# Moving a short normalisation chain on VectorE, and its transpose on TensorE, within a hand-ordered attention and routed-FFN kernel

## The chip, the cores and the metric

One core of a Trainium2 chip. The metric is device time in microseconds of one execution. The engines are named as in the profile: PE (TensorE), DVE (VectorE), ACT (ScalarE), POOL (GpSimd), SP (SyncE, which issues the transfers here).

## The reference

The input x has 16 batches of 512 tokens of 128 values. Two layers follow each other, and each is added to its input and normalised:

```
x = layernorm(x + attention(x))            # 16 heads of 8, causal, capped scores
x = layernorm(x + routed_ffn(x))           # 63 of 512 tokens per batch

# routed_ffn, for the chosen tokens of a batch:
weights = x @ router_w + router_b          # one weight for each token
k = 64; thr = 64th largest weight; sel_idx = sorted indices of the 63 largest
x_sel, w_sel, m_sel = rows of x, weights, mask at sel_idx
hn = rmsnorm(x_sel) * ln1
q, kk = rope(hn @ wq), rope(hn @ wk);  v = hn @ wv
o  = softmax(q kk^T / sqrt(8) + m_sel) v @ wo
x1 = x_sel + o
x2 = x1 + gelu((rmsnorm(x1) * ln2) @ w1) @ w2
out = x2 * w_sel scattered to sel_idx; the other tokens pass through
```

The change concerns the line of x2: the normalisation of x1 (the second rmsnorm of this layer), and how its result reaches the product with w1.

## The kernel before, in words

Batches are worked on in pairs. A pair has slots for 2 x 64 chosen tokens, so the small attention of the routed layer (track "att", one unit for each pair) fills 128 partitions. The main attention (scores, capped softmax, product with v) runs batch by batch, in 8 groups of two heads. The program is one loop over iterations, each with 16 steps, one group of the main attention to a step; a step has two halves. In each half PE first computes a unit of scores into the PSUM tile ps_s (line 1182), which ACT turns into probabilities (tanh line 716, exp line 731), POOL masks (line 627) and PE uses (line 1199, track "pv").

All other work is hung onto these halves by hand: PE_ORDER, VE_ORDER, POOL_ORDER and ACT_ORDER are tables of 32 entries, one for each half. An entry such as "att.h2T@-2" calls a function for the pair two iterations back; "/0" or "/1" picks the batch of a pair. Each engine goes through its own table in order, and the engines meet only at semaphores: every step counts up its track's semaphore, and whoever needs the step waits for the count. On DVE the halves mean nothing but the order.

The steps that matter here, in order of the data:

- att.wo (PE, line 1382) writes the attention's output projection into the PSUM tile ps_a. att.x1f (DVE, line 1073) adds the chosen tokens' own values. att.ss (line 1077) sums squares. att.root1 (guess, a, t: lines 806, 808, 809) and att.root2 (u2, u3, u4, y: lines 811 to 814) are an inverse root by polynomial on a 128x1 tile, sel_v. att.hn (line 1082) scales the tokens into the tile hn.
- att.h2T (PE, line 1387) turns hn into ps_a, DVE copies it, scaled, to the tile h2T (line 1085), and att.w1 (PE, line 1393) multiplies by w1. DVE copies that to hb (line 1091).
- route.wrow (PE, line 1206) spreads the token weights of a batch over all partitions of the PSUM tile ps_m; route.row (DVE, line 939) copies it to w_wide; route.win (DVE, line 946, four instructions) compares. This belongs to another batch.
- fin.root1 and fin.root2 (DVE, the same lines 806 to 814, on ln_v, 128x4) are the inverse root of a layer norm of yet another batch; fin.x1 (line 922) uses it.
- prep.xT (PE, line 1223) turns the 512 tokens of the next pair's first batch into ps_m, and DVE copies them to xT (line 828).

Two PSUM banks, ps_a and ps_m, are shared by all these steps. A table says whose reading must be over before a step may write:

```
    "att.h2T": ["att.x1f@0"],
    "att.w1": ["att.h2T@0"],
    "prep.xT/0": ["prep.vb/1@-1", "route.row/0@-2"],
```

So prep.xT of the first batch, which writes ps_m, waits until DVE's route.row has read ps_m. The chains on DVE wait for their own previous step by semaphore; the copy route.row waits for PE's wrow.

Of the kernel before, what the change touches and what calls it, by code (L numbers as in the profile page):

```python
# [61 lines left out]
def moments_of(tiles, tag=""):  # L62
# [48 lines left out]
    ["fin.y1T/1@-1"], ["att.P1@-2", "fin.yT/1@-1", "att.PV@-2"],  # L111
    [], ["fin.wo/1@-1"],
    ["pv.0/0@0", "pv.1/0@0", "pv.2/0@0"], ["att.oT@-2"],
    ["pv.3/0@0", "att.wo@-2", "route.wrow/0@-1"], ["att.h2T@-2"],
    [], ["prep.xT/0@1", "att.w1@-2"],
    ["route.won/0@-1", "prep.qk0/0@1", "prep.qk1/0@1"], ["fin.y0T/0@0", "pv.4/0@0", "route.wrow/1@-1"],
    ["pv.5/0@0", "pv.6/0@0"], ["route.thr/0@-1", "pv.7/0@0", "route.won/1@-1"],
    ["prep.v/0@1"], ["fin.y1T/0@0", "late.w2@-2"],
# [9 lines left out]
    ["prep.qk0/1@0", "fin.x1/0@-1", "route.coef/1@-2", "att.den@-2", "prep.qk1/1@0"], ["fin.yU1/1@-1"],  # L128
    ["att.PT0@-2", "prep.v/1@0", "prep.ss/1@0", "fin.y1/1@-1"], ["att.PT1@-2", "prep.root1/1@0"],
    ["prep.root2/1@0", "prep.qkn/1@0", "fin.yT/1@-1", "late.ln@-3", "prep.hi/1@0"], ["route.w/0@-1"],  # L130
    ["att.o@-2", "fin.res/1@-1", "att.oT@-2", "fin.ln/1@-1"], ["route.row/0@-1", "att.x1f@-2"],
    ["att.ss@-2", "fin.root1/1@-1", "att.root1@-2", "att.root2@-2", "att.hn@-2"],
    ["fin.root2/1@-1", "route.win/0@-1", "att.h2T@-2"],
    ["late.root1@-3", "fin.x1/1@-1", "prep.xT/0@1"], ["att.h@-2", "route.w/1@-1", "fin.yU0/0@0"],
    ["route.rank/0@-1", "prep.qk0/0@1", "prep.qk1/0@1", "fin.y0/0@0"], ["att.hp@-2"],
# [1326 lines left out]
```

How the kernel before makes its waits and increments, by code:

```python
    def wait(self, eng, unit, name):  # L312
        pair, k = self.where(unit)
        if not isinstance(pair, int) or 0 <= pair < PAIRS:
            eng.wait_ge(self.sems[k], pair * len(self.names) + (self.names.index(name) + 1))
# [190 lines left out]
        @block.sync  # L507
# [31 lines left out]
            def turn(b, k):  # L539
                if b.at_least(2):
                    sp.wait_ge(scores_ready, (b - 1).no * 16)
                for s, (dst, part) in enumerate(((q_st, "q"), (k_st, "k"))):
                    pl["prep"].wait(sp, b, f"lo_{part}")
                    sp.dma_start_transpose(out=dst[:, k].rearrange("p g (t n) -> p (g t) n", t=NT),
                                           in_=st[:, s].rearrange("p g t j c d -> p (g t j c d)")).then_inc(turned[k], 16)
# [17 lines left out]
                if live(p, PAIRS):  # L564
                    load_res(Batch(p, 1), 1)
                if live(p + 1, PAIRS):
                    turn(Batch(p, 2), 0)
                if p in (1, 2):
                    pe["sel"].wait(sp, p - 1, "R")
                    load_mask(2 * p if p == 1 else MASKS - 1, mask_a[:, :, :])
                    if p == 1:
                        load_mask(MASKS - 1, mask_b)
            for k in range(2):
                sp.wait_ge(out_stored[k], 16 * PAIRS)
# [2 lines left out]
        @block.gpsimd  # L577
# [30 lines left out]
            nc.gpsimd.memset(v_aug[:, :, :, :, :], 0.0).then_inc(zeroed, 1)  # L608
            nc.gpsimd.memset(pm[:, :, :], 0.0).then_inc(zeroed, 1)
            pool.wait_ge(zeroed, 2)
            for s in range(2):
```

## Time and profile before

| | |
|---|---|
| runs shown | 831.39, 833.25, 834.76 us; median 833.25 us |
| the profiled execution | span 830.0 us from first to last instruction; its own device time is not listed beside it |
| busy share of the span | PE 82%, DVE 72%, ACT 67%, PE weight loads 48%, POOL 47% |
| chain of work that ended last | PE 61%, DVE 18%, issue 10%, ACT 7%, POOL 3%, DMA 1% |
| pairs in the routed track | 8, one for each of 8 iterations |

The chain of work that ended last is followed back from the last instruction; its shares tell on which engine time could be won or lost. The busy shares are means over the whole span. The granted clock of PE is 1.00 where it runs at 2.4 GHz and 0.50 where it runs at 1.2 GHz. A row of a timeline gives start, duration, engine, line, operation, tiles, and in brackets how long the engine had stood idle before it and who released it. Where a row has a count over one, several instructions are merged, and the duration is from the start of the first to the end of the last.

### The profile page before, as it was taken

What the parts mean: (1) busy time and instruction counts of PE and PEld (TensorE: products, weight loads), DVE (VectorE), ACT (ScalarE), POOL (GpSimd) and SP (SyncE); (2) the same over time, 40 slices, a digit from 0 to 9 for tenths busy, and PEclk for the clock granted to TensorE, in tenths of its full rate; (3) what the DMA queues carried; (4) which work ended last, traced back from release to release, by engine and by line L of the source; (5) the groups of instructions that cost most, each with busy time, mean ns of one, the idle gap of its engine ahead of it and who ended that gap; (6) DMA issues with size and microseconds to landing.
All of it is one profiled execution on the core that took longest, in us unless ns stands there. A gap on an engine that the chain in (4) does not pass through costs nothing.

```text
span 830.0 us, 16995 instructions
## 1 busy us (share of the span) xinstructions
PE 678.9 (82%) x6576; PEld 401.4 (48%) x6576; DVE 595.4 (72%) x1681; ACT 554.2 (67%) x403; POOL 392.0 (47%) x399
## 2 busy tenths in 40 slices
PE   3588787889979988999899988998899879865652
PEld 2344334455546455645455545645565535434232
DVE  4442718777787788958888788769896986588455
ACT  0588688889768876959768876788687968600000
POOL 5263436447544574346455664446546543421201
PEclk8567678899789987989789987899799979985755
DMA  6321302033300503030304030120303030000001
GB/s 190 64 42 37 64 13 53 25 61 119 64 14 17 112 12 67 27 64 14 64 14 90 14 64 15 50 54 2 64 26 65 2 64 27 13 1 26 0 0 51
DMA packets 96913, 36.75 MB, mean 44 GB/s; under 512 B 68018, under 2 KB 94146, under 8 KB 96834
## 3 DMA queue, kind: packets, MB, share of 16 engines
q1 hardware_dynamic: 96834, 35.67, 18.8%
q8 instruction: 53, 0.87, 0.4%
q14 instruction: 26, 0.21, 0.1%
HBM read 14.69 MB, written 4.19 MB: 23 GB/s over the span
## 4 chain that ended last, share of the span: by engine, by line
PE 61%; DVE 18%; issue 10%; ACT 7%; POOL 3%; DMA 1%; POOLq 0%; DVEq 0%; ACTq 0%
PE ps_y L1199 16%; PE ps_s L1182 14%; ACT pr L731 4%; PE ps_m L1308 3%; PE ps_m L1230 3%; ACT th L716 3%; PE ps_m L1206 3%; PE ps_a L1230 3%; PE ps_m L1356 2%; PE ps_a L1393 2%; DVE v_aug L844 2%; PE ps_m L1258 2%; PE ps_a L1206 2%; PE ps_a L1258 1%; PE ps_a L1292 1%
## 5 line engine op out<-in xcount | busy, mean ns | idle before, releaser
L716 ACT ACTIVATE th<-ps_s 128x1024 f32<-128x1024 f32 (+1 forms) x256 | 280.2, 1129 | 110.7 <-PE ps_s L1182 102.0
L627 POOL TENSOR_TENSOR pr<-pr,tri 128x320 f32<-128x320 f32 (+1 forms) x256 | 194.8, 784 | 186.7 <-ACT pr L731 186.7
L731 ACT ACTIVATE pr<-th 128x2304 f32<-128x2304 f32 x128 | 271.5, 2122 | 15.5 <-PE ps_y L1199 15.4
L1182 PE MATMUL ps_s<-q_st,k_st 32*64 32x512 f16 (+7 forms) x2048 | 193.1, 319 | 24.9 <-ACT th L716 20.8
L1199 PE MATMUL ps_y<-pr,v_aug 128*32 128x512 f32 (+7 forms) x2048 | 157.4, 439 | 0.4 <-POOL pr L627 0.4
L1182 PEld LDWEIGHTS ps_s<-q_st,k_st 32*64 32x64 f16 x2048 | 92.3, 114 | 120.0 <-issue 54.3
L1199 PEld LDWEIGHTS ps_y<-pr,v_aug 128*32 128x32 f32 x2048 | 57.0, 113 | 66.9 <-issue 47.4
L641 POOL TENSOR_TENSOR st<-qk,st 128x1024 f16<-128x1024 f32 x32 | 73.8, 2327 | 32.3 <-DVE st L860 32.3
L629 POOL TENSOR_TENSOR k_wide<-qkT,head_of 128x1024 f32<-128x1024 f32 x16 | 30.1, 1902 | 58.0 <-DVE qkT L1029 58.0
L629 POOL TENSOR_TENSOR r<-x,rw_row 128x512 f32<-128x512 f32 x16 | 18.9, 1180 | 63.6 <-DVE x L922 63.6
L702 ACT ACTIVATE hq<-hu 128x512 f32<-128x512 f32 x8 | 5.0, 630 | 60.7 <-POOL hu L629 60.7
L629 POOL TENSOR_TENSOR st<-qk 128x1024 f32<-128x1024 f32 x16 | 30.3, 1892 | 20.0 <-DVE qk L833 19.9
L946 DVE SCALAR_TENSOR_TENSOR wins<-w_wide,x,later 128x512 f16<-128x512 f32 (+1 forms) x64 | 37.8, 590 | 2.5
L698 ACT ACTIVATE pm<-pm 128x1008 f32<-128x1008 f32 x8 | 8.3, 1038 | 42.8 <-DVE pm L1043 42.8
L629 POOL TENSOR_TENSOR z_base<-x,coef 128x512 f32<-128x512 f32 x16 | 18.2, 1136 | 36.9 <-DVE coef L970 36.9
L1308 PE MATMUL ps_m<-mask_a,E 128*64 128x512 f32 x112 | 30.3, 619 | 0.0
L870 DVE COPY y_u<-ps_y 128x512 f32<-128x512 f32 x32 | 21.7, 679 | 8.2 <-PE ps_y L1199 8.1
L844 DVE COPY v_aug<-ps_m 64x512 f32<-64x512 f32 x32 | 22.0, 689 | 7.3 <-PE ps_m L1238 6.8
L1230 PE MATMUL ps_m<-wT,xT 128*128 128x256 f32 x64 | 25.5, 537 | 0.9 <-DVE xT L828 0.9
L1230 PE MATMUL ps_a<-wT,xT 128*128 128x256 f32 x64 | 25.4, 538 | 0.8 <-DVE rank L953 0.8
L1387 PE MATMUL ps_a<-ident,hn 128*128 128x128 f32 x8 | 3.2, 396 | 26.3 <-DVE hn L1082 26.3
L833 DVE COPY qk<-ps_m 128x512 f32<-128x512 f32 x16 | 11.0, 688 | 18.0 <-PE ps_m L1230 18.0
(220 smaller groups left out, 1133.9 us busy)
## 6 DMA issues: line engine op xcount, KB each, us to landing
x_in<-in_L_attn_x SPq DMA_DIRECT2D x16, 256.0 KB, 2.8
x_res<-in_L_attn_x SPq DMA_DIRECT2D x16, 256.0 KB, 3.1
result<-y_out SPq DMA_DIRECT2D x16, 256.0 KB, 2.4
mask_a<-in_L_ffn_attention_mask SPq DMA_DIRECT2D x3, 1024.0 KB, 5.2
pr<-in_L_ffn_attention_mask SPq DMA_DIRECT2D x2, 1024.0 KB, 8.6
w_sb<-in_L_ffn_w SPq DMA_DIRECT2D x2, 256.0 KB
q_st<-st SPq DMA_TRANSPOSE x16, 4.5
k_st<-st SPq DMA_TRANSPOSE x16, 4.7
```

The costliest lines, as they stand in the source:

```text
L627: return nc.gpsimd.tensor_tensor(buf, buf, tri[:, None, :].to_broadcast([P, blocks, 64]), ALU.mult)
L629: mul = lambda out, a, b: nc.gpsimd.tensor_tensor(out, a, b, ALU.mult)
L641: pl["prep"].done(nc.gpsimd.tensor_tensor(lo_parts[s], qk_twice[s], hi_parts[s], ALU.subtract), f"lo_{part}", b)
L716: nc.scalar.activation(th[:, gi % 2, c0:c1], ps_s[:, c0:c1], ACT.Tanh, scale=1.0 / (QK_SCALE ** 2 * DH ** 0.5 * SOFTCAP))\
L731: nc.scalar.activation(pr[:, probs_at(n):probs_at(n) + GROUP], th[:, gi % 2, :], ACT.Exp, scale=SOFTCAP).then_inc(exp_done, 1)
L844: ve["prep"].done(nc.vector.tensor_copy(v_aug[rows, k].rearrange("p b n c -> p (b n) c")[:, :, 16 * s:16 * s + DH], at("prep.v", b)[rows, ...
L946: step(lambda: nc.vector.scalar_tensor_tensor(won[c], w_wide[:, P * c:], x1[:, k, c, D:D + 1], later[:, 0:n], ALU.is_le, ALU.mult, accum_o ...
L1182: last = mm(ps_s[64 * s:64 * s + 64, COL[kb]:COL[kb] + S - 64 * kb], k_st[rows, k, gi // 2, 64 * kb:64 * kb + 64], q_st[rows, k, gi // 2, ...
L1199: last = mm(ps_y[32 * j:32 * j + 32, 64 * kb:S], v_aug[:, k, kb, gi, :], pr[:, c:c + S - 64 * kb], start=(kb == 0), stop=(kb == NB - 1), s ...
L1206: last = tr(bank[:, P * c:P * c + P], src(c), ident[:, :])
L1230: last = mm(at(f"prep.qk{i}", b)[:, :].rearrange("p (n t e) -> p n t e", t=2, e=32)[:, :, t % 2], xT[:, P * t:P * t + P], wT[:, 0:2, :].re ...
L1308: last = mm(at("sel.R")[SLOTS * k:SLOTS * k + SLOTS, :], E[:, c, SLOTS * k:SLOTS * k + SLOTS], (mask_b if k and q < 2 else mask_a)[:, c, : ...
```

## The change

Two tables are edited, nothing else. In VE_ORDER, route.row and fin.root1 go behind the whole chain from att.x1f to att.hn; before, route.row stood ahead of att.x1f, and fin.root1 between att.ss and att.root1. In PE_ORDER, prep.xT goes from the second half of step 7 to the second half of step 6, and att.h2T from there to the first half of step 7; att.w1 stays.

```diff
--- before.py
+++ after.py
@@ -111,8 +111,8 @@
-    ["pv.3/0@0", "att.wo@-2", "route.wrow/0@-1"], ["att.h2T@-2"],
-    [], ["prep.xT/0@1", "att.w1@-2"],
+    ["pv.3/0@0", "att.wo@-2", "route.wrow/0@-1"], ["prep.xT/0@1"],
+    ["att.h2T@-2"], ["att.w1@-2"],
@@ -128,8 +128,8 @@
-    ["att.o@-2", "fin.res/1@-1", "att.oT@-2", "fin.ln/1@-1"], ["route.row/0@-1", "att.x1f@-2"],
-    ["att.ss@-2", "fin.root1/1@-1", "att.root1@-2", "att.root2@-2", "att.hn@-2"],
+    ["att.o@-2", "fin.res/1@-1", "att.oT@-2", "fin.ln/1@-1"], ["att.x1f@-2", "att.ss@-2"],
+    ["att.root1@-2", "att.root2@-2", "att.hn@-2", "route.row/0@-1", "fin.root1/1@-1"],
```

DVE before, from the copy of the weights row (line 939) on; sel_v is the 128x1 tile of the tokens' root, ln_v the 128x4 tile of the other root:

```order
L939 COPY w_wide<-ps_m 128x512
L1073 TENSOR_TENSOR x1f<-xs,ps_a 128x128
L1077 ISA hn,sel_v<-x1f 128x128
L1077 ISA sel_v 128x1
L806 TENSOR_SCALAR ln_v<-ln_v 128x4
L808 TENSOR_TENSOR ln_v<-ln_v 128x4
L809 TENSOR_TENSOR ln_v<-ln_v 128x4
L806 TENSOR_SCALAR sel_v<-sel_v 128x1
L808 TENSOR_TENSOR sel_v<-sel_v 128x1
```

DVE now, from the same place on:

```order
L1073 TENSOR_TENSOR x1f<-xs,ps_a 128x128
L1077 ISA hn,sel_v<-x1f 128x128
L1077 ISA sel_v 128x1
L806 TENSOR_SCALAR sel_v<-sel_v 128x1
L808 TENSOR_TENSOR sel_v<-sel_v 128x1
L809 TENSOR_TENSOR sel_v<-sel_v 128x1
L811 SCALAR_TENSOR_TENSOR sel_v<-sel_v 128x1
L812 SCALAR_TENSOR_TENSOR sel_v<-sel_v 128x1
L813 SCALAR_TENSOR_TENSOR sel_v<-sel_v 128x1
L814 SCALAR_TENSOR_TENSOR sel_v<-sel_v 128x1
L1082 TENSOR_SCALAR hn<-x1f,sel_v 128x128
L939 COPY w_wide<-ps_m 128x512
```

The copy and the three ln_v instructions have gone behind line 1082; what follows them (fin.root2, route.win, the copy to h2T) has kept its order.

PE before, from the end of a unit of scores (line 1182) to the product with w1 (line 1393):

```order
L1387 MATMUL ps_a<-ident,hn 128x128
L1182 MATMUL ps_s<-q_st,k_st 64x512 x2
L1182 MATMUL ps_s<-q_st,k_st 64x448 x2
L1182 MATMUL ps_s<-q_st,k_st 64x64 x2
L1182 MATMUL ps_s<-q_st,k_st 64x384 x2
L1182 MATMUL ps_s<-q_st,k_st 64x128 x2
L1182 MATMUL ps_s<-q_st,k_st 64x320 x2
L1182 MATMUL ps_s<-q_st,k_st 64x192 x2
L1182 MATMUL ps_s<-q_st,k_st 64x256 x2
L1223 MATMUL ps_m<-ident,x_in 128x128 x4
L1393 MATMUL ps_a<-h2T,w_sb 128x128 x4
```

PE now, the same stretch:

```order
L1223 MATMUL ps_m<-ident,x_in 128x128 x4
L1182 MATMUL ps_s<-q_st,k_st 64x512 x2
L1182 MATMUL ps_s<-q_st,k_st 64x448 x2
L1182 MATMUL ps_s<-q_st,k_st 64x64 x2
L1387 MATMUL ps_a<-ident,hn 128x128
L1182 MATMUL ps_s<-q_st,k_st 64x384 x2
L1182 MATMUL ps_s<-q_st,k_st 64x128 x2
L1182 MATMUL ps_s<-q_st,k_st 64x320 x2
L1182 MATMUL ps_s<-q_st,k_st 64x192 x2
L1182 MATMUL ps_s<-q_st,k_st 64x256 x2
L1393 MATMUL ps_a<-h2T,w_sb 128x128 x4
```

The transposes of x_in have come to the head of the stretch, and the transpose of hn (line 1387) stands between the two units of scores that it preceded.

## Rows read from the trace of the kernel before

**Rows 1.** The page, busy time of the two engines, share, instructions

```profile
PE 678.9 (82%) x6576; PEld 401.4 (48%) x6576; DVE 595.4 (72%) x1681; ACT 554.2 (67%) x403; POOL 392.0 (47%) x399
```

**Rows 2.** Waits: who waited for whom, us in total, times, longest

```profile
PE ps_a L1387 <- DVE hn L1082: 26.3, 8, 3.8
PE ps_a L1393 <- DVE h2T L1085: 6.6, 5, 2.8
```

**Rows 3.** Timeline of PE around the step, second pair

```profile
313.66 0.49 PE L1382 MATMUL ps_a<-wo,oT 128*128 128x128 f32 x2
313.98 0.60 PE L1206 MATMUL ps_m<-ident,x 128*128 128x128 f32 x4
314.51 0.73 PE L1182 MATMUL ps_s<-q_st,k_st 32*64 32x384 f16 x10
318.54 0.33 PE L1387 MATMUL ps_a<-ident,hn 128*128 128x128 f32 x1 [3.29 <-DVE hn L1082]
318.80 1.18 PE L1182 MATMUL ps_s<-q_st,k_st 32*64 32x512 f16 x16
319.90 1.12 PE L1223 MATMUL ps_m<-ident,x_in 128*128 128x128 f32 x4
321.83 2.04 PE L1393 MATMUL ps_a<-h2T,w_sb 128*128 128x128 f32 x8 [0.81 <-DVE h2T L1085]
```

**Rows 4.** Timeline of DVE in the same place

```profile
314.62 0.69 DVE L939 COPY w_wide<-ps_m 128x512 f32<-128x512 f32 x1 [0.77 <-PE ps_m L1206]
315.23 0.28 DVE L1073 TENSOR_TENSOR x1f<-xs,ps_a 128x128 f32<-128x128 f32 x1
315.65 0.42 DVE L1077 CUSTOM_DVE_ANT_0 hn<-x1f 128x128 f32<-128x128 f32 x1
316.00 0.54 DVE L806 TENSOR_SCALAR ln_v<-ln_v 128x4 int32<-128x4 int32 x1
316.86 0.14 DVE L806 TENSOR_SCALAR sel_v<-sel_v 128x1 int32<-128x1 int32 x1
318.20 0.29 DVE L1082 TENSOR_SCALAR hn<-x1f,sel_v 128x128 f32<-128x128 f32 x1
318.40 0.16 DVE L811 SCALAR_TENSOR_TENSOR ln_v<-ln_v 128x4 f32<-128x4 f32 x1
321.34 0.35 DVE L1085 TENSOR_SCALAR h2T<-ps_a,g 128x128 f32<-128x128 f32 x1
```

**Rows 5.** Timeline of POOL there; then DVE in the sixth pair

```profile
315.06 1.45 POOL L627 TENSOR_TENSOR pr<-pr,tri 128x320 f32<-128x320 f32 x2 [2.61 <-ACT pr L731]
...
674.49 0.54 DVE L806 TENSOR_SCALAR ln_v<-ln_v 128x4 int32<-128x4 int32 x1
```

**Rows 6.** Timelines of DVE and POOL where a root's chain meets a mask

```profile
187.14 0.73 DVE L809 TENSOR_TENSOR ln_v<-ln_v 128x4 f32<-128x4 f32 x1
187.90 0.52 DVE L811 SCALAR_TENSOR_TENSOR ln_v<-ln_v 128x4 f32<-128x4 f32 x1
188.45 0.16 DVE L812 SCALAR_TENSOR_TENSOR ln_v<-ln_v 128x4 f32<-128x4 f32 x1
...
186.97 1.44 POOL L627 TENSOR_TENSOR pr<-pr,tri 128x320 f32<-128x320 f32 x2 [2.76 <-ACT pr L731]
```

**Rows 7.** Timeline of DVE in the last pair: the same chain without the other work

```profile
803.20 0.29 DVE L1073 TENSOR_TENSOR x1f<-xs,ps_a 128x128 f32<-128x128 f32 x1 [0.89 <-PE ps_a L1382]
803.63 0.29 DVE L1077 CUSTOM_DVE_ANT_0 hn<-x1f 128x128 f32<-128x128 f32 x1
803.97 0.15 DVE L806 TENSOR_SCALAR sel_v<-sel_v 128x1 int32<-128x1 int32 x1
805.32 0.29 DVE L1082 TENSOR_SCALAR hn<-x1f,sel_v 128x128 f32<-128x128 f32 x1
```

**Rows 8.** Windows: us, busy PE, PEld, DVE, ACT, POOL, granted clock, DMA

```profile
309.60:319.80 10.20, 6.91 (x102) 3.93 (x94) 7.04 (x32) 7.75 (x6) 4.31 (x5) 1.00 0.65 129
319.80:330.10 10.30, 9.49 (x52) 6.34 (x49) 9.31 (x27) 4.84 (x4) 5.48 (x7) 0.50 0.09 25
```

## The prediction

> **What bounds the kernel now.** I read the page first: PE is the busiest engine, 679 of 830 us, DVE next with 595 [rows 1]. So an idle stretch of PE is lost time unless another engine was late anyway. The view of waits then says where PE idles in the place that the change edits: 26.3 us in eight waits for the tokens' normalised tile, hn, and 6.6 us in five waits one step on, for the turned and scaled copy h2T [rows 2]. The timelines of one pair show how the two hang together. PE ends the output projection at 314.15 and its scores at 315.24, then stands still for 3.29 us until DVE has hn; after that come 16 score matmuls and the transposes of x_in, and another 0.81 us of waiting for h2T before w1 [rows 3]. On DVE the reader is to see a chain with almost no gap: from the copied weights row at 314.62 to the copy of h2T at 321.34, DVE stands idle only 0.77 us, ahead of the weights row [rows 4]. And DVE's copy of h2T stands behind everything that the change reorders. So in this stage DVE's order of work, not PE's, says when w1 can start: PE's second wait ends last, and what PE gains at the first one it can lose at the second.
>
> **The change part by part.** No instruction is added or removed; no DMA moves in any table. I follow the second pair, then multiply.
>
> PE's side. The first thing behind the scores is now the transposes of x_in. They write the bank that the weights row is read from, so they wait for that copy, and the copy now stands behind hn. PE's first wait is thus for hn plus the copy, not for hn.
>
> DVE's start. The chain no longer waits for the weights row on PE (ends 314.58), only for the projection (ends 314.15). The copy started 0.04 us after its release [rows 3, 4], so x1f starts at 314.19. That is 0.43 us of idle time won.
>
> Two chains laid end to end. Before, the other root's three instructions lay between the sum of squares and the tokens' root. There they cost less than they will alone: from x1f to the tokens' first root step is 0.77 us where nothing lies between [rows 7], against 1.63 us with three in between, of which one took 0.54 instead of about 0.16 [rows 4, 6]; without those 0.38, and without the 0.13 by which the sum of squares was longer (0.42 against 0.29 [rows 4, 7]), it is 1.12, so the three cost 0.35. Behind the copy they cost three times 0.195 us, the spacing of dependent steps (805.32 less 803.97 over seven steps [rows 7]), 0.585. That is 0.24 lost.
>
> The mask on POOL. This is the term that decides the sign. The 0.54 us instruction ended as POOL's two mask instructions ended: they run from 315.06 to 316.51, it from 316.00 to 316.54 [rows 4, 5]. Elsewhere a root's chain met the same pair of mask instructions whole: the instruction in hand ended 0.90 us after POOL's start (187.87 less 186.97), the next one 1.45 us after it (188.42), each held for the rest of a POOL instruction, and the third was free again with 0.16 [rows 6]. Rows of DVE that read PSUM are not held so: x1f ran during the mask in 0.28 us, against 0.29 in the last pair [rows 4, 7]. Before the change the copy of the weights row and x1f, which both read PSUM, covered most of the mask, and only the end of it was paid: 0.38 + 0.13. Now the small steps, which read SBUF alone, stand there. With x1f at 314.19, the first root step starts at 314.96, the next at 315.15, 0.09 us after POOL began. By rows 6 that one ends at 315.06 + 0.90 = 315.96 and the one behind it at 315.06 + 1.45 = 316.51. The next step starts at 316.55, three more and then hn follow at 0.195 each: hn starts at 316.55 + 0.78 = 317.33. The copy starts 0.20 later (318.40 less 318.20 [rows 4]), at 317.53, and ends 0.69 later, 318.22. PE's transposes start at 318.26, where its wait ended at 318.54 before: the first wait goes from 3.29 to 3.02 us, not more. The other root starts 0.61 behind the copy's start (315.23 less 314.62), at 318.14, and its second part 0.585 later, at 318.73. Before, that part started at 318.40 [rows 4]. Everything behind it is unchanged, so the copy of h2T starts 0.33 us late, at 321.67, and w1 at 322.16.
>
> [...]
>
> PE between the two waits. From 318.26 PE has the transposes, two units of scores and the transpose of hn, at most 1.12 + 1.18 + 0.33 and twice that for the scores if the clock is already low [rows 3, 8]: done by 322.1, so DVE's copy at 321.67 plus 0.35 and 0.14 (321.83 less 321.69) still ends last. ACT gets its scores no later than before by more than that 0.33. The transposes moved earlier free the x_in tile earlier, and SP reloads it earlier; nobody needs it for an iteration.
>
> The sum. The 0.54 us stands in five of the eight pairs, first at 316.00, last at 674.49 [rows 4, 5]: five times +0.33 is +1.65 us. In the last pair there is no copy and no other root, so nothing changes. In the first and the seventh the mask lies elsewhere; I take 0, between -0.7 (free of the mask, below) and +0.5. Bounds for the five: if the mask is missed altogether, x1f 314.19, hn 316.31, copy 316.51, other root 317.12, its second part 317.71 against 318.40, so -0.69 each, -3.5 in all; if the mask catches one step more, 0.2 more each, +2.7 in all. I take +1.65, because rows 6 are the same instructions against the same mask. The sum stands on the span of 830.0, giving 831.7; the median of the runs lies 3.25 above that span, and I carry the difference over: 834.9 us.
>
> **The rivals.** First, the chain slips past the mask: DVE's steps are not held, because POOL comes later or yields. For it: x1f starts early enough that one step is done before 315.06. Against it: five steps are not. It gives -3.5, 829.8 us.
>
> Second, PE's clock. In the 10.2 us from 309.6 PE has its full clock, 2.4 GHz; behind the 3.29 us stall it is granted 0.50, 1.2 GHz, for 10.3 us [rows 8]. If a wait cut to 3.02 or less no longer brings that fall, PE's 9.5 us of work there shrink to half. But DVE is busy 9.31 of those 10.30 us, so at most 1.0 us a pair is to be had: -5 over five pairs, 828.3, and less if the first rival holds as well. Against it: 0.27 us less idle time, and a second idle stretch, of up to 1.9 us, close behind. [...]
>
> Third, slower: the low clock lasts longer. Two waits of 3.0 and up to 1.9 us now lie with little work between, where 0.81 stood before. If each low stretch lasts a third longer, 3.4 us more at half clock, and PE is the bound by then, each costs 1.7 us: five times that and the 1.65 give 843. It decides only if the clock is still low beyond the point where DVE's 9.3 us are done; a part of it gives 838 to 840.
>
> Fourth, the change does not do what it says: the wait for hn merely becomes one for the copy and the end of the stage does not move, 833.2 us.
>
> **How the numbers follow.** Forecast 0.55, chain past the mask 0.13, full clock 0.13, longer low clock 0.12, nothing moves 0.07. Half a per cent, 4.2 us, is about what a measurement of this kernel can tell from no change; the limits are 829.1 and 837.4. Faster: 0.10 of the clock's case, 0.04 of the first rival, 0.02 of the forecast, 0.16. Slower: 0.10 of the longer low clock, 0.07 of the forecast, whose own range is 831.5 to 838; 0.17. The rest, 0.67, is within. The range takes in the clock's case below and a part of the longer low clock above: 827.5 to 840.
>
> **What would show it.** In the timeline after: x1f 0.04 us behind the projection; one step of lines 808 to 814 on sel_v lasting about 0.8 us and the next about 0.5, ending with POOL's mask; the transposes of x_in waiting about 3.0 us, with the copy of line 939 as releaser; w1 waiting longer than before, about 1.5 to 2 us where the clock is high. The prediction is wrong if those steps last 0.16 us, if the clock stays at 1.00 behind this stage, or if w1 starts earlier against the projection than the 7.68 us (321.83 less 314.15) of before.

## The result

The kernel after takes 847.85 us (median of 4 runs, 847.28 to 849.68), the kernel before 832.33 us in the same comparison (4 runs, 831.39 to 834.76). The ratio is 1.0191, 95% interval [1.017, 1.0213]: slower by 1.9%, outside the forecast's 827.5 to 840 us. The profiled execution took 847.88 us, its span is 846.0 us, 16.0 longer than before.

The page after, busy time of the engines, answers to [rows 1]:

```profile
PE 693.7 (82%) x6576; PEld 409.2 (48%) x6576; DVE 601.0 (71%) x1681; ACT 554.8 (66%) x403; POOL 391.1 (46%) x399
```

PE does the same 6576 instructions in 14.8 us more busy time. So most of the loss isn't idle time: PE worked more slowly. The waits after, of the same steps as [rows 2] (who waited for whom, total us, times, longest):

```profile
PE ps_m L1223 <- DVE w_wide L939: 15.6, 6, 3.1
PE ps_a L1393 <- DVE h2T L1085: 10.5, 6, 4.0
...
PE ps_a L1387 <- DVE hn L1082: 6.2, 3, 2.9
```

These three waits are 32.3 us together; the two of before were 32.9. So the idle time at the place that was edited hardly changed. The timeline of PE there, second pair, answers to [rows 3]:

```profile
313.32 0.49 PE L1382 MATMUL ps_a<-wo,oT 128*128 128x128 f32 x2
...
314.18 0.73 PE L1182 MATMUL ps_s<-q_st,k_st 32*64 32x384 f16 x10
317.99 0.63 PE L1223 MATMUL ps_m<-ident,x_in 128*128 128x128 f32 x4 [3.08 <-DVE w_wide L939]
318.55 0.62 PE L1182 MATMUL ps_s<-q_st,k_st 32*64 32x512 f16 x6
319.10 0.33 PE L1387 MATMUL ps_a<-ident,hn 128*128 128x128 f32 x1
319.36 1.07 PE L1182 MATMUL ps_s<-q_st,k_st 32*64 32x384 f16 x10
321.78 1.62 PE L1393 MATMUL ps_a<-h2T,w_sb 128*128 128x128 f32 x6 [1.35 <-DVE h2T L1085]
```

And of DVE, which answers to [rows 4]:

```profile
313.85 0.29 DVE L1073 TENSOR_TENSOR x1f<-xs,ps_a 128x128 f32<-128x128 f32 x1 [0.33 <-PE ps_a L1382]
314.28 0.29 DVE L1077 CUSTOM_DVE_ANT_0 hn<-x1f 128x128 f32<-128x128 f32 x1
...
314.61 0.15 DVE L806 TENSOR_SCALAR sel_v<-sel_v 128x1 int32<-128x1 int32 x1
314.80 0.80 DVE L808 TENSOR_TENSOR sel_v<-sel_v 128x1 f32<-128x1 f32 x1
315.63 0.51 DVE L809 TENSOR_TENSOR sel_v<-sel_v 128x1 f32<-128x1 f32 x1
316.18 0.16 DVE L811 SCALAR_TENSOR_TENSOR sel_v<-sel_v 128x1 f32<-128x1 f32 x1
...
316.96 0.28 DVE L1082 TENSOR_SCALAR hn<-x1f,sel_v 128x128 f32<-128x128 f32 x1
317.16 0.68 DVE L939 COPY w_wide<-ps_m 128x512 f32<-128x512 f32 x1
```

POOL's mask in the same place, as in [rows 5]:

```profile
314.73 1.41 POOL L627 TENSOR_TENSOR pr<-pr,tri 128x320 f32<-128x320 f32 x2 [2.73 <-ACT pr L731]
```

The reader is to see the predicted collision: the steps of 0.80 and 0.51 us end 0.87 and 1.41 us after the mask began (314.73), as in [rows 6] (0.90 and 1.45). From the projection's end, 313.81, w1 starts 7.97 us later; before it was 7.68, and the forecast said 8.01 (322.16 less 314.15).

**Where the 16 us are.** I cut both traces at the end of each pair's projection (line 1382, "wo") and list from one to the next. The low stretches are those at granted clock 0.50, written as the begin behind the projection + the length, in us. What PE does at the two clocks, the trace of before shows in its scores (line 1182, f16): at 1.00 a matmul of 64 columns takes 0.188 us and one of 448 columns 0.348 (from 318.8 us on), at 0.50 they take 0.256 and 0.576 (from 323.8 on). The 384 columns more take 0.160 and 0.320 us, which is 2.4 and 1.2 columns a ns; the figures in GHz ahead of the result stand for no more than that.

| from the projection of | before | low stretches | after | low stretches |
|---|---|---|---|---|
| first pair | 87.6 | 4.6+6.8, 76.2+6.8 | 87.7 | 4.7+10.2, 76.4+6.8 |
| second | 93.2 | 5.7+10.2, 36.4+10.2, 77.4+10.2 | 91.8 | 5.8+10.2, 36.5+6.8, 80.9+6.8 |
| third | 87.9 | 4.7+10.2, 76.4+6.8 | **99.1** | **2.7+17.1, 30.0+20.5**, 88.0+6.8 |
| fourth | 89.9 | 5.6+10.2, 36.3+6.8, 80.7+3.4 | 93.5 | 2.6+13.7, 36.7+10.2, 77.7+10.2 |
| fifth | 87.6 | 4.5+10.2, 76.2+6.8 | 87.9 | 4.7+10.2, 76.4+6.8 |
| sixth | 70.3 | 5.6+10.2 | 70.2 | 5.6+10.2 |
| seventh | 60.2 | -3.3+23.9, 27.5+6.8, 41.1+45.9 | 62.9 | 0.3+23.9, 27.6+10.2, 44.6+45.1 |

All low stretches together are 284.8 us before and 321.5 after. The third pair loses 11.2 us, the fourth 3.6, the seventh 2.7, and the second gains 1.3. The third pair's projection even ends 1.7 us sooner than before (405.64 against 407.30); 0.3 of that it had already at the second projection.

The windows of the third pair after (us, busy PE, PEld, DVE, ACT, POOL, granted clock, DMA share, GB/s):

```profile
408.30:425.40 17.10, 15.46 (x80) 9.02 (x80) 13.41 (x42) 8.97 (x7) 8.16 (x8) 0.50 0.06 17
435.70:456.20 20.50, 20.45 (x112) 15.14 (x114) 14.82 (x39) 9.53 (x7) 5.69 (x6) 0.50 0.10 27
```

Then the same pair's windows before; the second of them at full clock:

```profile
412.00:422.20 10.20, 10.20 (x56) 6.79 (x57) 9.65 (x29) 5.69 (x5) 5.10 (x6) 0.50 0.09 26
...
437.00:457.00 20.00, 18.86 (x198) 11.51 (x198) 15.92 (x51) 16.66 (x13) 10.91 (x10) 1.00 0.43 92
```

PE is busy for 20.45 of the 20.50 us from 435.7, and DVE for 14.82: PE is the bound there. Like for like, the same 112 matmuls, counted in both traces from the product with w2 on, took 20.63 us here (435.75 to 456.38) and 12.86 before (434.36 to 447.22). That is 7.8 of the pair's 11.2 us. Another 3.0 were lost ahead of it: that product begins 30.1 us behind the projection, before it was 27.1.

How the third pair came to it stands in the timeline after, all engines, from 431 us on. In it, lo_v is the 128x8 tile of another layer norm's root (late.root2), v_aug holds the values of a batch still to come, which DVE copies out of ps_m, and line 1400 is late.w2, the product with w2. It writes ps_m, so it waits for that copy.

```profile
432.34 0.17 DVE L811 SCALAR_TENSOR_TENSOR lo_v<-lo_v 128x8 f32<-128x8 f32 x1 [0.25 <-issue]
...
432.51 1.41 POOL L627 TENSOR_TENSOR pr<-pr,tri 128x320 f32<-128x320 f32 x2 [2.73 <-ACT pr L731]
...
432.54 0.86 DVE L812 SCALAR_TENSOR_TENSOR lo_v<-lo_v 128x8 f32<-128x8 f32 x1
...
433.43 0.52 DVE L813 SCALAR_TENSOR_TENSOR lo_v<-lo_v 128x8 f32<-128x8 f32 x1
...
434.09 1.41 DVE L844 COPY v_aug<-ps_m 64x512 f32<-64x512 f32 x2
...
435.75 2.05 PE L1400 MATMUL ps_m<-w_sb,hu 128*128 128x128 f32 x8 [2.07 <-DVE v_aug L844]
```

Before, the same instructions:

```profile
432.18 0.17 DVE L812 SCALAR_TENSOR_TENSOR lo_v<-lo_v 128x8 f32<-128x8 f32 x1
432.38 0.17 DVE L813 SCALAR_TENSOR_TENSOR lo_v<-lo_v 128x8 f32<-128x8 f32 x1
...
432.69 1.41 DVE L844 COPY v_aug<-ps_m 64x512 f32<-64x512 f32 x2
...
433.48 1.41 POOL L627 TENSOR_TENSOR pr<-pr,tri 128x320 f32<-128x320 f32 x2 [2.31 <-ACT pr L731]
...
434.36 1.13 PE L1400 MATMUL ps_m<-w_sb,hu 128*128 128x128 f32 x8 [1.09 <-DVE v_aug L844]
```

Why DVE is late there stands a few us earlier on its timeline after:

```profile
422.94 0.36 DVE L877 RECIPROCAL rd<-ps_a 128x32 f32<-128x32 f32 x1 [1.52 <-PE ps_a L1206]
...
425.72 0.69 DVE L939 COPY w_wide<-ps_m 128x512 f32<-128x512 f32 x1 [1.63 <-PE ps_m L1206]
```

And before:

```profile
423.56 0.36 DVE L877 RECIPROCAL rd<-ps_a 128x32 f32<-128x32 f32 x1 [0.77 <-PE ps_a L1206]
...
425.13 0.69 DVE L939 COPY w_wide<-ps_m 128x512 f32<-128x512 f32 x1
```

The first low stretch lasts to 425.4 after (422.2 before), and DVE waits for PE's transposes twice, 1.52 and 1.63 us, where it waited 0.77 us and not at all. So late, another root's chain (lo_v) meets POOL's mask and is held 1.04 us (0.86 and 0.52 for twice 0.17). The copies into v_aug begin 1.40 us later than before, PE waits 2.07 us instead of 1.09, and there its clock falls again (0.50 from 435.7 us on).

### The profile page after: what moved, and what is told of

Its sections match the earlier page's. It is cut to its first block, busy times and chain, and to the rows that moved or that the text cites. A ratio compares the mean times of both kernels' runs of the same rounds, so it can differ in the third digit from the quotient of the medians.

```text
span 846.0 us, 16995 instructions
## 1 busy us (share of the span) xinstructions
PE 693.7 (82%) x6576; PEld 409.2 (48%) x6576; DVE 601.0 (71%) x1681; ACT 554.8 (66%) x403; POOL 391.1 (46%) x399
## 4 chain that ended last, share of the span: by engine, by line
PE 61%; DVE 18%; issue 9%; ACT 7%; POOL 3%; DMA 1%; POOLq 0%; DVEq 0%; ACTq 0%
PE ps_y L1199 16%; PE ps_s L1182 14%; ACT pr L731 4%; PE ps_m L1308 3%; PE ps_m L1230 3%; ACT th L716 3%; PE ps_a L1230 3%; PE ps_m L1206 2%; PE ps_m L1356 2%; PE ps_a L1393 2%; DVE v_aug L844 2%; PE ps_m L1258 2%; PE ps_a L1206 2%; PE ps_a L1258 1%; PE ps_a L1292 1%
## 5 line engine op out<-in xcount | busy, mean ns | idle before, releaser
L731 ACT ACTIVATE pr<-th 128x2304 f32<-128x2304 f32 x128 | 271.5, 2122 | 13.5 <-PE ps_y L1199 13.5
L1182 PE MATMUL ps_s<-q_st,k_st 32*64 32x512 f16 (+7 forms) x2048 | 196.0, 321 | 27.5 <-ACT th L716 23.5
L1199 PE MATMUL ps_y<-pr,v_aug 128*32 128x512 f32 (+7 forms) x2048 | 161.7, 448 | 0.4 <-POOL pr L627 0.4
L629 POOL TENSOR_TENSOR k_wide<-qkT,head_of 128x1024 f32<-128x1024 f32 x16 | 30.1, 1902 | 61.3 <-DVE qkT L1029 61.3
L1393 PE MATMUL ps_a<-h2T,w_sb 128*128 128x128 f32 x64 | 16.4, 437 | 10.8 <-DVE h2T L1085 10.5
```

Source lines behind the costliest of these rows:

```text
L629: mul = lambda out, a, b: nc.gpsimd.tensor_tensor(out, a, b, ALU.mult)
L731: nc.scalar.activation(pr[:, probs_at(n):probs_at(n) + GROUP], th[:, gi % 2, :], ACT.Exp, scale=SOFTCAP).then_inc(exp_done, 1)
L1182: last = mm(ps_s[64 * s:64 * s + 64, COL[kb]:COL[kb] + S - 64 * kb], k_st[rows, k, gi // 2, 64 * kb:64 * kb + 64], q_st[rows, k, gi // 2, ...
L1199: last = mm(ps_y[32 * j:32 * j + 32, 64 * kb:S], v_aug[:, k, kb, gi, :], pr[:, c:c + S - 64 * kb], start=(kb == 0), stop=(kb == NB - 1), s ...
```

## The experiments

Letters in the expectations: C is the clock taken simply (the wait behind the projection makes it fall, and filling that wait pays), D is DVE's new order costing by itself, A is alignment (where a pair stands decides when the clock falls and rises, so small shifts move long stretches). The letters P, S, T, U, L, M and N are explained where they first stand. What was measured, with the third pair's period read from each trace as above; ratios are to the kernel before on the same chip, with 95% intervals:

| run | us | ratio | third pair |
|---|---|---|---|
| DVE's half of the change | 849.71 | 1.0162 [1.0089, 1.0235] | 99.0 |
| PE's half | 832.32 | 0.9973 [0.9931, 1.0016] | 87.9 |
| after, first wait filled | 848.60 | 1.0129 [1.0029, 1.0229] | 99.0 |
| before, first wait filled | 852.03 | 1.0192 [1.0106, 1.0277] | 98.5 |
| after, third pair 1.6 us later | 834.87 | 1.0016 [0.9991, 1.0041] | 88.7 |
| before, third pair 2.2 us later | 849.17 | 1.0143 [1.0061, 1.0226] | 98.9 |
| before, pairs 2 to 6 delayed 1.35 us | 835.12 | 1.0007 [0.9982, 1.0032] | 91.1 |
| after, the same | 850.77 | 1.0202 [1.014, 1.0264] | 99.0 |
| DVE's half, the same | 849.51 | 1.0203 [1.0188, 1.0218] | 98.9 |
| PE's half, the same | 838.93 | 1.0067 [1.0043, 1.009] | 89.7 |
| before, h2T's copy first | 846.06 | 1.0129 [1.0063, 1.0194] | 98.9 |
| the same with PE's half | 854.01 | 1.0263 [1.0236, 1.029] | 98.7 |
| after, v_aug's wait filled | 834.24 | 1.0026 [1.0012, 1.004] | 88.8 |
| before, v_aug's wait filled | 831.40 | 0.9984 [0.9971, 0.9997] | 87.9 |
| h2T's copy first, PE's half, v_aug's wait filled | 840.55 | 1.0094 [1.0079, 1.0109] | 88.6 |
| the same, both waits filled | 847.91 | 1.0203 [1.017, 1.0236] | 92.0 |
| after, v_aug's wait filled in the third pair alone | 845.57 | none given | 95.7 |
| after, copies to v_aug ahead of the root | 847.17 | 1.0201 [1.017, 1.0232] | 92.1 |

The period is that of the one execution that was profiled, which need not be the median run: it took 858.49 us in "before, first wait filled" (median 852.03), 856.16 in the kernel after with all delays (850.77), and 852.41 in "after, first wait filled", whose four runs were 844.41, 844.78, 852.41 and 853.26. Where a line has been put into a kernel, the lines behind it have higher numbers: late.w2 stands in line 1400 or 1407.

**Which half does it.** First, the change's DVE lines alone, on PE's old table:

```diff
-    [..., "fin.ln/1@-1"], ["route.row/0@-1", "att.x1f@-2"],
-    ["att.ss@-2", "fin.root1/1@-1", "att.root1@-2", "att.root2@-2", "att.hn@-2"],
+    [..., "fin.ln/1@-1"], ["att.x1f@-2", "att.ss@-2"],
+    ["att.root1@-2", "att.root2@-2", "att.hn@-2", "route.row/0@-1", "fin.root1/1@-1"],
```

> Only DVE's order is changed, PE's is that of before. Theory C (the loss is PE's low clock, which lasts longer because the transposes of x_in now wait for the copied weights row with PE empty, so that PE idles 3.1 us, and then again 1.2 us with little work between): here PE waits for hn alone, which DVE has 1.5 us earlier than before, so the idle stretch shrinks from 3.3 to about 2.4 us and the time stays within 826 to 836 us, low-clock total at or under the 285 us of before. Theory D (the loss is DVE's: the mask and the two roots laid end to end make each pair late, and that adds up): DVE's order is that of the changed kernel, so it must be slow too, 843 us or more.

Measured: w1 7.98 us behind the projection, third pair 99.0 us with low stretches at 2.7 (17.1 long) and 30.0 (20.5), all as in the kernel after. The time is that of D (843 or more), not of C (826 to 836). DVE's half is the whole of it.

The PE lines alone:

```diff
-    [..., "route.wrow/0@-1"], ["att.h2T@-2"],
-    [], ["prep.xT/0@1", "att.w1@-2"],
+    [..., "route.wrow/0@-1"], ["prep.xT/0@1"],
+    ["att.h2T@-2"], ["att.w1@-2"],
```

> Only PE's order is changed, DVE's is that of before: the weights row is copied first, so the transposes of x_in find their bank free, and they and a unit of scores fill the time in which PE waited for hn. Theory C: the idle stretch of 3.3 us becomes two of about 1.9 us, the clock is low no longer than before, 822 to 836 us. Theory D: DVE's chain is as before, so 829 to 836 us as well. A third theory, P (PE's new order alone brings the second idle stretch and with it the longer low clock): 843 us or more.

Measured: no difference, w1 at 7.69 us. So P is out. In the second pair PE's wait for hn is cut to 1.7 us and what it saves is waited one step on, 2.3 us for h2T. That PE gains at the first wait what it loses at the second was right.

**Filling the wait behind the projection.** Three matmuls of 128x512 ahead of the transposes of x_in (kernel after) or of hn's transpose (before), pairs 1 to 6, into a bank overwritten later:

```diff
-    [..., "route.wrow/0@-1"], ["prep.xT/0@1"],
+    [..., "route.wrow/0@-1"], ["att.fill@-2", "prep.xT/0@1"],
...
+            def att_fill(q, _):
+                if q > 5:
+                    return
+                bank_free("att.h2T", q)
+                for _i in range(3):
+                    mm(ps_a[:, :], w1_sb[:, 0:P], w1_sb[:, :], start=True, stop=True)
```

> The changed kernel with three more matmuls of 128x512 in float32 on each of the first six pairs, into a PSUM tile that is overwritten later, ahead of the transposes of x_in: they keep PE busy for about 2.6 us of its 3.0 us wait and add nothing to the result. Theory C: the clock no longer falls there, the low-clock total drops from 322 to under 285 us, and the time falls to 820 to 835 us. Theory D: PE's filled wait changes nothing for DVE, 847 us or slightly more.

> The kernel before with the same three matmuls ahead of the transpose of hn, in its 3.3 us wait. Theory C: the clock stays up behind that wait too; DVE is busy 9.3 of the 10.3 us there, so the gain is at most some 5 us: 822 to 831 us, and the difference to the changed kernel with the same filling shrinks to the 1 to 4 us that DVE's order costs. Theory D: no change to before, 832 us.

Measured: the fall is only put off, in pairs 2 to 5 from 2.6 to 5.8 us behind the projection to 8.1 to 9.4 (kernel after), and from 4.5 to 5.7 to 12.4 to 12.8 (before). The kernel after gains nothing that can be measured, though all its low stretches together are now 301 us for 321.5. The kernel before now has 95.8, 98.5, 96.0 and 95.6 us in pairs 2 to 5 and loses 1.9%, which neither C (822 to 831) nor D (832) foresaw. Theory C falls: less idle time and a later fall are worth nothing, or less, if the low stretch then lies in work that PE's speed decides.

**Moving the third pair alone.** One delay on PE, ahead of the third pair's oT: 832 columns in the kernel after, 1192 in the kernel before. The expectations put them at 1.4 and 2.0 us; measured, the second pair became 1.6 and 2.2 us longer (93.4 for 91.8, 95.4 for 93.2 us):

```diff
-    ["pv.0/0@0", "pv.1/0@0", "pv.2/0@0"], ["att.oT@-2"],
+    ["pv.0/0@0", "pv.1/0@0", "pv.2/0@0", "att.pad@-2"], ["att.oT@-2"],
...
+            def att_pad(q, _):
+                n = {2: 832}.get(q, 0)
+                if n:
+                    bank_free("att.oT", q)
+                while n:
+                    m = min(n, F)
+                    mm(ps_m[:, 0:m], w1_sb[:, 0:P], w1_sb[:, 0:m], start=True, stop=True)
+                    n -= m
```

> The changed kernel with one delay: two matmuls (512 and 320 columns, float32, some 1.4 us, written where the next step writes anyway, without effect on the result) ahead of the third pair's transpose of its attention output. Theory A (alignment: the 0.3 us that DVE is late per pair matters little; it shifts the work against the moments at which the clock is withdrawn and granted, so that in the third pair the clock falls 2.7 us behind the projection instead of 4.7 and a second long low stretch follows): 1.4 us later the third pair meets the clock as before did, its way to the fourth takes some 88 us instead of 99, and the whole 833 to 840 us, faster with work added. Theory D (DVE's new order itself brings the long low stretches): the delay adds to the time, 848 to 850 us.

> The kernel before with the same kind of delay, some 2.0 us (three matmuls, 1192 columns), ahead of the third pair's transpose of its attention output, so that this pair meets the clock as the changed kernel's did. Theory A: its way to the fourth pair takes some 99 us instead of 88 and the whole 843 to 852 us, with neither order changed. Theory D: 832 to 836 us, the delay alone.

Measured: with 1.6 us of work more the kernel after is 13 us faster, as fast as before; with 2.2 us more the kernel before is as slow as after in three of its four runs (the fourth took 840.68 us), with the third pair at 98.9 us and its second low stretch at 29.8 us. Its first is 5.9+13.7 where the kernel after has 2.7+17.1: alike are the ends, 19.5 and 19.8 us behind the projection. The windows of the first (columns as above):

```profile
412.60:422.80 10.20, 9.82 (x53) 6.14 (x51) 9.56 (x30) 5.87 (x5) 5.10 (x6) 0.50 0.09 26
422.80:460.00 37.20, 34.57 (x394) 20.53 (x394) 30.49 (x93) 28.98 (x21) 17.45 (x16) 1.00 0.24 51
```

After 10.2 us of low clock the clock stays at 1.00 through the stretch that the kernel after spends at 0.50. The order is the same and the 16 us are gone, so what makes them is how the third pair meets the clock, and not the order by itself.

**A delay in every pair.** The same function with 672 columns (measured 1.35 us) in pairs 2 to 6, in four kernels:

```diff
-                n = {2: 832}.get(q, 0)
+                n = {1: 672, 2: 672, 3: 672, 4: 672, 5: 672}.get(q, 0)
```

On the kernel before:

> The kernel before with a delay of some 1.13 us (672 columns) in each of the second to sixth pairs at the same place, so that each pair arrives against the clock as the first and third did, whose way to the next took 87.6 and 87.9 us, the second's and fourth's 93.2 and 89.9. Theory A: five ways of about 88.8 us in place of 446.1 us in all, 828 to 833 us in spite of 5.7 us of added work. Theory D: before plus up to 5.7 us, 835 to 839 us.

On the kernel after:

> The changed kernel with the same delays in the second to sixth pairs. Theory A: no pair meets the long low stretches, and against the kernel before with the same delays only DVE's lateness of 0.3 us a pair is left, some 1 to 3 us: 829 to 837 us. Theory D: 848 to 854 us.

On DVE's half alone:

> DVE's new order, PE's old one, and the delays of the two padded kernels (672 columns in each of the second to sixth pairs). With all pairs delayed alike the old orders took 835 and the new ones 851 us, so alignment is not all. Theory S (split run: the low clock is given back early where PE goes from the transposes of x_in straight into w1, as in the old orders; DVE's lateness opens a gap ahead of w1, and PE's new order puts scores between): here the gap of about 0.9 us stands ahead of w1, so 845 us or more. Theory T (only PE's new order, the transposes far ahead of w1, holds the clock low): 833 to 839 us.

On PE's half alone:

> PE's new order, DVE's old one, and the same delays. Theory S: the transposes lie 5 us ahead of w1, in the wait for hn, so that the low clock lasts where a pair meets it late: 842 us or more. Theory U (only DVE's new order costs, the PE order is free, as it was without delays at 832): 833 to 838 us.

Measured: 835.12, 850.77, 849.51 and 838.93 us. The kernel before bears 6.8 us of added work with no change that can be measured. The first two numbers are those of D (835 to 839 and 848 to 854), not of A, and DVE's half alone came out as S said. The two with DVE's new order still fall into long pairs (99.0, 95.4, 94.8 us and 98.9, 94.9 us); PE's half alone has one (94.9 us), and its time lies between the two forecasts. So a single shift isn't a cure: DVE's new order comes to the slow case more easily, but neither order is safe. A sign of it: in the third pair, with the delays, the clock falls 3.3 us behind the projection in the kernel after and 3.5 in the kernel before, and comes back after 17.1 us and after 6.8. Why is not shown. The kernel before, unedited, took 838.44 to 843.29 us in four of 13 runs on one chip, and 839.36 and 841.54 in two of 19 on another; none of these was profiled.

**Getting w1 earlier.** DVE copies h2T ahead of route.win, on the kernel before, then with PE's half as well:

```diff
-    ["fin.root2/1@-1", "route.win/0@-1", "att.h2T@-2"],
+    ["fin.root2/1@-1", "att.h2T@-2", "route.win/0@-1"],
```

> The kernel before with one edit on DVE: the copy of h2T goes ahead of the four instructions of route.win, so w1 no longer waits for them. From the projection to w1 about 6.9 us where the clock is high, instead of 7.7, and 7.7 where it is low, since PE then comes straight from the transposes. DVE's work stays the same, so it gains at most 0.3 us a pair. Theory A, alignment: the time can go either way by a low stretch, 822 to 848 us; without alignment it would be 829 to 833.

> The same edit on DVE with PE's new order: the transposes of x_in fill the wait for hn, and w1 comes at about 5.5 us behind the projection, 2.2 us earlier than before. PE's idle time in the stage falls from 4.1 to about 2.5 us, but DVE's chain up to the copy of w1's result is as long as before. 820 to 845 us by alignment; if PE's idle time in this stage alone counted, 822.

Measured: in pairs 2 to 5 w1 starts 6.7 to 7.7 us and 5.4 to 5.8 us behind the projection, up to 2.3 us earlier than before, and both are slower, 846.06 us (one of its four runs took 836.39) and 854.01, outside the 820 to 845 forecast. They have pairs of 98.9 and 96.6, and of 98.7, 96.1 and 95.5 us. A shorter stage bought nothing.

**The wait for v_aug.** In the 14 traces up to here I took PE's wait ahead of late.w2 (for v_aug) in pairs 2 to 5, 56 in all, against the pair's period:

| wait for v_aug, us | pairs | period, us |
|---|---|---|
| 0.69 to 0.77 | 20 | 87.6 to 92.0 |
| 1.05 to 1.15 | 16 | 87.9 to 93.5, once 95.4 (delayed 2.2) |
| 1.29 to 1.37 | 5 | 95.5 to 96.9 |
| 1.67 to 1.71 | 6 | 94.8 to 96.1 |
| 1.90 to 2.10 | 9 | 98.5 to 99.1 |

So a longer wait goes with a longer pair. The moment at which the clock first comes back sorts the same pairs as well. In the 20 pairs of the three lower rows PE's first low stretch (two of them are split) ended 19.2 to 20.6 us behind the projection, whether it had begun at 2.7 us or at 12.8; in the 36 others it ended by 16.3, but for one (19.5, in the kernel after with its first wait filled, 92.0 us). It fits that filling the first wait bought nothing: in the third pair of the kernel after the fall was put off from 2.7 to 9.4 us, and the clock came back at 19.6 instead of 19.8. What sets that moment was not tested.

To see whether the wait is a cause, two matmuls were put into it, in pairs 1 to 6, first in the kernel after, then before:

```diff
-    ["prep.v/0@1"], ["fin.y1T/0@0", "late.w2@-2"],
+    ["prep.v/0@1"], ["fin.y1T/0@0", "late.fill@-2", "late.w2@-2"],
...
+            def late_fill(q, _):
+                if q > 5:
+                    return
+                ve["fin"].wait(t_, Batch(q + 2, 0), "yU1")
+                for _i in range(2):
+                    mm(ps_y[:, :], w1_sb[:, 0:P], w1_sb[:, :], start=True, stop=True)
```

> The kernel after, with two matmuls of 128x512 (about 1.7 us of TensorE work, overwritten later) put where TensorE waits 2.07 us for v_aug ahead of late.w2, in pairs 1 to 6. Theory A (a late rise of the clock loses time because the wait for v_aug then lets it fall a second time): the stretch of low clock that began 30 us behind the third pair's projection is gone or much shorter, the third pair's period is 88 to 92 us instead of 99.1, the whole 836 to 842 us. Rival L (the late rise of the first stretch costs by itself, and the second fall only accompanies it): the period stays at 97 or more and the whole is 847 to 853 us. Rival M (the fall only moves to the next wait): the second stretch starts 3 to 12 us later and lasts as long, the period stays within 2 us of 99.

> The same two matmuls in the kernel before, whose third pair waits 1.09 us for v_aug and keeps its clock there: the control. Theories A and L: 833 to 838 us (0 to 0.9 us of work too much in each of six pairs), periods 87.5 to 93.5. Rival M: a stretch of low clock appears later in some pair, and the whole is 840 or more.

Measured: 834.24 us. With this wait filled the kernel after runs its first five pairs in 88.6 to 88.8 us each, all with the same two low stretches (4.6 to 4.7 and 72.9 us behind the projection in the second to the fifth, 10.2 long). That is slightly under the 836 to 842 that A gave. But the third pair came to its place another way, and its late rise didn't occur, so this didn't test the link itself. The control, at 831.40 us, is a little under the 833 to 838 of A and L and 0.16% under the kernel before, the lowest median of all kernels here, if by less than such a measurement can tell well; one of its pairs took 92.6 us with the wait filled.

The same fill where w1 was earliest (h2T's copy first, with PE's half), the first diff; then with two matmuls ahead of hn's transpose as well, the second:

```diff
-    ["prep.v/0@1"], ["fin.y1T/0@0", "late.w2@-2"],
+    ["prep.v/0@1"], ["fin.y1T/0@0", "late.fill@-2", "late.w2@-2"],
```

```diff
-    ["att.h2T@-2"], ["att.w1@-2"],
+    ["att.fill@-2", "att.h2T@-2"], ["att.w1@-2"],
```

> The order with h2T's copy ahead of route.win and the changed TensorE order (854.01 us, w1 5.4 us behind the projection), with the two matmuls in the wait for v_aug. Theory A: periods of 98.7, 96.1 and 95.5 us fall to 86 to 90, and the 2.3 us by which w1 is earlier are then seen: 815 to 835 us. Rivals L and M: 848 to 858 us.

> As the run before, with two matmuls also in TensorE's wait ahead of hn's transpose. If the fall at the projection is what the rest follows from, filling both waits leaves no stretch of low clock until later in a pair: 810 to 832 us. Rivals L and M: the fall is put off (as it was with three matmuls there) and the whole stays at 845 to 856 us.

Measured: 840.55 us, 13.5 under the same kernel without the fill, but not the 815 to 835 that A gave: two pairs stay at 93.2 us. With both waits filled it is 847.91, as L and M said, and that with 278 us of low clock in all, less than the 284.8 of the kernel before. So the sum of the low stretches doesn't decide, but what work lies in them. With w1 5.4 to 6.2 us behind the projection in pairs 2 to 5, up to 2.3 us earlier, neither kernel is faster than before.

Then the fill in the third pair alone, which leaves everything up to that wait as it is in the kernel after:

```diff
-                if q > 5:
+                if q != 2:
```

> The kernel after with the two matmuls of 128x512 ahead of late.w2 in the third pair alone, so that it comes to that pair as the kernel after does: projection done at 405.6 us, the clock low from 2.7 us behind it for 17.1 us, DVE late, and the 2.07 us wait for v_aug filled. Theory A (the second fall is the loss): no stretch of low clock begins 30 us behind the third projection, that pair's period falls from 99.1 to 88 to 93 us, and the whole is 836 to 843 us. Rival L (the late rise costs by itself): 97 us or more, and 847 to 851 us. Rival M (the second fall is only put off): a long stretch begins within 12 us after it, the period is 95 to 99, the whole 844 to 849 us.

Its four runs took 844.44, 846.70, 846.87 and once 831.57 us, too far apart for an interval; the profile is of the first. Its other pairs repeat the kernel after (87.7, 91.8, 93.5, 87.9 us, with the same low stretches), so that the third can be compared. The windows of the third pair:

```profile
408.30:425.30 17.00, 15.46 (x79) 9.01 (x80) 13.34 (x41) 8.88 (x7) 8.14 (x8) 0.50 0.06 17
425.30:445.80 20.50, 18.03 (x227) 11.97 (x225) 18.84 (x47) 18.20 (x14) 6.04 (x9) 1.00 0.10 27
445.80:452.70 6.90, 6.50 (x28) 4.11 (x30) 4.91 (x16) 1.22 (x1) 3.56 (x2) 0.51 0.06 16
```

The timeline of PE, at the filled wait (lines 1401 and 1407) and at the next one, ahead of late.sc1, the multiplication by x and ET:

```profile
433.43 1.88 PE L1401 MATMUL ps_y<-w_sb 128*128 128x512 f32 x4
435.68 1.13 PE L1407 MATMUL ps_m<-w_sb,hu 128*128 128x128 f32 x8 [0.36 <-DVE v_aug L844]
...
446.20 1.19 PE L1416 MATMUL ps_m<-x,ET 64*128 64x128 f32 x4 [2.51 <-issue]
```

And of DVE ahead of that next wait:

```profile
442.48 0.29 DVE L812 SCALAR_TENSOR_TENSOR qn_v<-qn_v 128x128 f32<-128x128 f32 x1
442.81 0.29 DVE L813 SCALAR_TENSOR_TENSOR qn_v<-qn_v 128x128 f32<-128x128 f32 x1
443.13 0.83 DVE L814 SCALAR_TENSOR_TENSOR qn_v<-qn_v 128x128 f32<-128x128 f32 x1
...
445.42 0.68 DVE L888 COPY yT<-ps_m 128x512 f32<-128x512 f32 x1
```

The 17 us low stretch is there as in the kernel after, the wait for v_aug is 0.36 us, and the fall 30 us behind the projection is gone: in this execution that wait causes it. But the period falls only to 95.7 us, a third of the way (3.4 of 11.2): DVE is still late, the next root (qn_v, 128x128) meets the next mask, PE waits 2.51 us one step on (1.11 before, ahead of the same multiplication), and the clock falls there. The view names no releaser for that wait ("issue"), but the kernel's table has late.sc1 wait for the copy of yT, and PE starts 0.10 us behind that copy's end (446.10). That is rival M's mechanism and its numbers, only the new low stretch is short, 6.8 us.

Last, the wait taken away by order, no work added:

```diff
-    ["route.rank/1@-1", "late.root2@-3", "prep.v/0@1"],
+    ["route.rank/1@-1", "prep.v/0@1", "late.root2@-3"],
```

> The kernel after with one entry moved on DVE: the copies into v_aug (1.41 us) stand ahead of late.root2's four instructions (0.17 us each, and up to 0.86 where they meet POOL's mask) in place of behind them. No work is added. Theory A: TensorE's wait for v_aug shrinks by 0.8 to 1.9 us, to under 0.5 us in every pair, no stretch of low clock begins there, periods are 86 to 90 us, and the whole is 825 to 836 us. Rival L or M: the third pair keeps 95 us or more and the whole is 842 to 850 us. Rival N (late.root2, four instructions later, delays what needs it): the wait goes, but DVE's later copies come 0.8 us later for TensorE, and the whole is within 3 us of 847.

Measured: 847.17 us. The wait for v_aug goes to 0.49 to 0.93 us in pairs 2 to 5, and the next one grows to 2.77 in the third pair, where a root again met a mask (POOL's began at 444.82). The timeline of PE there, then DVE's step:

```profile
448.71 1.24 PE L1409 MATMUL ps_m<-x,ET 64*128 64x128 f32 x8 [2.77 <-issue]
```

```profile
444.90 0.93 DVE L812 SCALAR_TENSOR_TENSOR qn_v<-qn_v 128x128 f32<-128x128 f32 x1
```

The periods of the second to the fifth pair are 95.7, 92.1, 92.2 and 92.2 us: rival N, by its number and its mechanism. What DVE is late with in one place it owes in the next. And the loss is of another kind here: PE is busy 680.1 us, near the 678.9 of the kernel before, so what was lost is idle time, where the kernel after lost it to the clock (693.7).

## Why the prediction was wrong

**The local steps held.** x1f starts 0.04 us behind the projection, as said. The held steps end 0.87 and 1.41 us after POOL's start (0.90 and 1.45 said); hn starts 3.11 us behind x1f (3.14); the first wait is 3.08 us (3.02), the second 1.35 (less than the 1.5 to 2 said); w1 starts 7.97 to 7.98 us behind the projection in each of the five pairs that hold the collision, against 7.68 to 7.71. The term forecast at +0.33 measured +0.27 to +0.30, some +1.4 us over five pairs (+1.65 said). The moved steps that took 0.80 and 0.51 us ended at 315.60 and 316.14, POOL's two mask instructions at 315.59 and 316.14; lo_v's 0.86 and 0.52 us ended at 433.40 and 433.95, the mask's at 433.37 and 433.92. Why a step beside the mask lasts that long, no run shows.

**The step that failed is the sum.** It carried five local terms straight to the end of the span: "five times +0.33 is +1.65 us", then "the span of 830.0, giving 831.7". Behind w1 it so put everything at nothing. What lies there is not only work but also the clock at which PE does it. The low stretches were taken with the lengths and places of the kernel before, 10.3 us behind each stall [rows 8]. They vary: in the second pair two later ones were 6.8 us long instead of 10.2, the third pair came to its projection 1.7 us early, its clock fell 2.7 us behind the projection instead of 4.7 and came back after 17.1 us instead of 10.2. From there the delay runs through DVE to PE's wait for v_aug, and behind that the same 112 matmuls took 20.63 us instead of 12.86. The pair became 11.2 us longer, where the sum had 0.33.

**The third rival was the right family, mis-sized.** It said that a longer low clock decides once it outlasts DVE's 9.3 us, and that happened. Its price was 1.7 us in every pair; measured was 11.2 in one pair, 3.6 in the next and nothing in others, because most of the cost (7.8 of the 11.2 us) lies not in the longer stretch but in the later fall that follows from it. And 0.12 was too small a chance: [rows 8] showed a stage where PE's 9.49 and DVE's 9.31 us of work stand about even, so that either can be made the bound by a small shift, and the trace of before already held pairs of 87.6 and of 93.2 us with the same work. I had followed one of them, and none of the three signs named as proof against the forecast came: they all looked at the edited place.

**The drain.** "In the last pair ... nothing changes" is right of the last pair's chain, but from the seventh projection to the eighth it took 2.7 us more, beside a low stretch that began 3.6 us later. It is not there in two kernels with the same DVE order and the delays in pairs 2 to 6 (60.2 and 60.3 us). Its cause stays open.

**What is shown and what is not.** Shown: DVE's half alone makes the loss; most of it is PE doing the same work at granted clock 0.50; a shift of the third pair by 1.6 or 2.2 us takes it away or brings it; in the execution with its third pair filled, PE's 2.07 us wait is what causes the second fall; taking that fall away returns 3.4 of 11.2 us, and the next wait takes over. Not shown: what fixes the first fall at 2.7 or 4.7 us behind the projection and the moment of its end, how 0.3 us of DVE's lateness shortened the second pair's low stretches, why DVE's new order stays slow with all pairs delayed, and why the run filled in the third pair alone once took 831.57 us.

## What to carry to other kernels

Where two engines' loads in a stage are about even and PE's clock falls in that stage, a local term of 0.3 us can't be added to the end: list the low stretches and the period of every pass first, and if passes of equal work differ (87.6 and 93.2 us here), give the range their spread. Before explaining a small reordering by its own place, delay one pass by a microsecond or two, in the kernel before as well; if that alone moves the time as much as the change does (1.4 and 1.7% here, against 1.9), how the passes meet the clock is a part of what was measured. Then delay all passes as well: here the new order stayed slow under that. Shorter waits and an earlier product are no gain by themselves, unless the wait that ends up last is followed too.

## What the runs showed of the hardware that was not expected

- More work was faster: 1.6 us of matmuls took 13 us off the kernel after (847.85 to 834.87), and two matmuls in each of six pairs about as much (834.24). The same kind of work put 16 us on the kernel before (849.17).
- PE's clock came back after 10.2 us in one pair and after 17.1 in another, behind stalls of nearly the same length (3.0 to 3.1 us in the first, the third and the fourth pair of the kernel after, with low stretches of 10.2, 17.1 and 13.7). A wait of 0.99 us ahead of late.sc1 was followed by a fall in the second pair of the kernel before (36.4 us behind the projection), and one of 1.11 us by none in the third.
- Steps on 128x8 and 128x128 tiles are held by POOL's mask like those on 128x4: 0.86 and 0.52 us for 0.17, 0.83 and 0.93 for 0.29. Steps of a single element per partition, whose own time is 0.16, are held as long (0.80 and 0.51).
